# GRU layers: input weights combined on the chip, and PSUM sums with the column as the outer index

## The reference, cut to what matters

```
xn   = layernorm(x) * g + b                      # 96 channels
x_inner, z = split(xn @ w_in.T)                  # 192 + 192
gx   = x_inner @ wih.T + bih                     # for each of 4 GRUs, 3 gates of 96
step: gh = h @ whh.T + bhh
      r, u = sigmoid(gx_r + gh_r), sigmoid(gx_u + gh_u)
      n = tanh(gx_n + r * gh_n);  h = (1 - u) * n + u * h
y    = silu(fwd + bwd) * silu(z)
out  = x + y @ w_out.T
```

## Time and profile before

| | |
|---|---|
| median of 3 runs | 1262.82 us (1260.11 to 1264.99) |
| profiled execution, time | 1265.31 us |
| profiled execution, span in the profile | 1263.5 us |
| mean granted TensorE clock | 0.58 of 2.4 GHz |
| TensorE matmuls busy | 1142.3 us (90%) |
| VectorE busy | 943.2 us (75%) |
| ScalarE busy | 670.5 us (53%) |
| POOL busy | 129.8 us (10%) |

### The profile page before, as it was taken

One profiled execution on the slowest core, in us unless ns is written; L12 is line 12 of the kernel. 1 busy time (PEld: TensorE's weight loads), 2 busy tenths in 40 slices (PEclk: granted clock), 3 DMA queues, 4 the chain that ended last, 5 costly groups with the idle time before them and its releaser, 6 DMA issues. The chain is left out here.

```text
span 1263.5 us, 60733 instructions
## 1 busy us (share of the span) xinstructions
PE 1142.3 (90%) x24696; PEld 991.4 (78%) x24696; DVE 943.2 (75%) x5715; ACT 670.5 (53%) x4263; POOL 129.8 (10%) x100
## 2 busy tenths in 40 slices
PE   3778799748999999999999967999999999999995
PEld 2545254344999999999999964799999999999985
DVE  4553799964777777777777785677777777777776
ACT  4223601016666666666666652666666666666663
POOL 1001299740000000000000002000000000000000
PEclk8587799957555555555555555755555555555555
DMA  4000000000000000000000000000000000000000
GB/s 115 2 12 1 31 28 27 27 19 1 5 4 4 4 4 4 4 4 4 4 4 4 5 2 7 3 4 4 4 4 4 4 4 5 4 4 4 4 4 26
DMA packets 7955, 12.94 MB, mean 10 GB/s; under 512 B 5649, under 2 KB 6833, under 8 KB 7384
## 3 DMA queue, kind: packets, MB, share of 16 engines
q1 hardware_dynamic: 7674, 9.06, 2.3%
HBM read 8.27 MB, written 0.79 MB: 7 GB/s over the span
## 5 line engine op out<-in xcount | busy, mean ns | idle before, releaser
L1107 PE MATMUL L3s_early<-L3s_h_hi,L_w_hidden 97*128 97x8 f16 x4096 | 200.2, 175 | 4.9 <-DVE L3s_h_hi L1019 4.0
L1107 PE MATMUL L2s_early<-L2s_h_hi,L_w_hidden 97*128 97x8 f16 x4096 | 200.2, 176 | 4.8 <-DVE L2s_h_hi L1019 4.1
L1107 PEld LDWEIGHTS L3s_early<-L3s_h_hi,L_w_hidden 97*128 97x128 f16 x4096 | 163.7, 109 | 26.2 <-DVE L3s_h_hi L1019 7.8
L1107 PEld LDWEIGHTS L2s_early<-L2s_h_hi,L_w_hidden 97*128 97x128 f16 x4096 | 163.7, 109 | 25.9 <-DVE L2s_h_hi L1019 7.4
L1019 DVE TENSOR_TENSOR_SCAN L3s_h_hi<-L3s_renew,L3s_terms 96x32 f16<-96x32 f32 x512 | 113.2, 221 | 85.2 <-ACT L3s_terms L1059 59.4
L1019 DVE TENSOR_TENSOR_SCAN L2s_h_hi<-L2s_renew,L2s_terms 96x32 f16<-96x32 f32 x512 | 113.1, 221 | 85.2 <-ACT L2s_terms L1059 59.4
L1059 ACT ACTIVATE L2s_terms<-L2s_cand 96x16 f32<-96x16 f32 x512 | 111.7, 218 | 93.8 <-DVE L2s_cand L1004 62.4
L1059 ACT ACTIVATE L3s_terms<-L3s_cand 96x16 f32<-96x16 f32 x512 | 111.7, 218 | 93.7 <-DVE L3s_cand L1004 62.7
L1053 ACT ACTIVATE L2s_reset<-L2s_early 96x16 f32<-96x16 f32 x512 | 92.6, 181 | 68.3 <-PE L2s_early L1107 62.7
L1053 ACT ACTIVATE L3s_reset<-L3s_early 96x16 f32<-96x16 f32 x512 | 92.6, 181 | 68.2 <-PE L3s_early L1107 62.6
L1107 PE MATMUL L3s_early<-L3s_h_lo,L_w_hidden 96*128 96x8 f16 x2048 | 127.3, 171 | 0.1
(11 more groups left out here) (229 smaller groups left out, 2884.5 us busy)
## 6 DMA issues: line engine op xcount, KB each, us to landing
L_w_input_raw<-in_L_wih SPq DMA_DIRECT2D x2, 1164.0 KB
l_w_raw<-in_L_w SPq DMA_DIRECT2D x1, 1296.0 KB
L_w_hidden_raw<-in_L_whh SPq DMA_DIRECT2D x2, 582.0 KB
stream<-in_x SPq DMA_DIRECT2D x2, 384.0 KB, 3.6
out<-stream SPq DMA_DIRECT2D x4, 192.0 KB, 2.1
l_idft<-in_idft SPq DMA_DIRECT2D x1, 400.0 KB
rpe_lw<-in_rpe_lw SPq DMA_DIRECT2D x1, 384.0 KB
l_dft<-in_dft SPq DMA_DIRECT2D x1, 288.0 KB, 3.0
```

The lines of the kernel that those rows point to most:

```text
L1107: return e.matmul(dst, weights.hidden[0:rows, wp, GATES * (2 * g + j) + gate, :], rhs, start=False, stop=False, skip_group_check=True)
```

## The change

The input projection and the GRUs' input weights are both linear, so their product is made once per layer: `inner` (192 by 96) times `wih` gives weights that act on the normalised input directly. TensorE makes that product at the start of `gru_input`, in three PSUM banks with two fp32 products each. ScalarE rounds a bank to fp16, TensorE subtracts the rounded part with a product by minus the identity, and ScalarE rounds what is left. `forward` and `backward` hold the normalised input, with 96 channels instead of 192, so 36 input products per eight steps remain of the 72. All three kinds of sum, and `xT`, `forward`, `gate` and `y` too, have the column (batch) as outer and the step as inner index. `WeightSplit` rounds only the recurrent weights and a row of biases; the loads ask for 96 rows and for the 97th apart.

```diff
 class WeightSplit:
     def load(self, e, d):
-        for raw, name, _ in self.raw:
-            e.dma_start(raw[:], d[name]).then_inc(self.loaded, 16)
+        e.dma_start(self.hidden_raw[0:C], d[f"{self.layer}_whh"][0:C]).then_inc(self.loaded, 16)
+        e.dma_start(self.hidden_raw[C:C + 1], d[f"{self.layer}_whh"][C:C + 1]).then_inc(self.loaded, 16)
+        e.dma_start(self.bias_raw[C:C + 1], d[f"{self.layer}_bih"]).then_inc(self.loaded, 16)
+        e.dma_start(self.weights.raw[:], d[f"{self.layer}_wih"]).then_inc(self.weights.raw_loaded, 16)
+        e.dma_start(self.weights.inner[:], d[f"{self.layer}_w_inner"]).then_inc(self.weights.raw_loaded, 16)
     def lo(self, e):
-        for i, (raw, _, parts) in enumerate(self.raw):
-            e.wait_ge(self.hi_ready, i + 1)
-            e.tensor_tensor(parts[:, 1], raw[:], parts[:, 0], ALU.subtract).then_inc(self.lo_ready, 1)
+        e.wait_ge(self.hi_ready, 1)
+        e.tensor_tensor(hidden[:, 1], self.hidden_raw[:], hidden[:, 0], ALU.subtract).then_inc(self.lo_ready, 1)
+        e.wait_ge(self.hi_ready, 2)
+        e.wait_ge(self.lo_ready, 1)
+        e.tensor_tensor(bias[:, 1], self.bias_raw[C:C + 1], bias[:, 0], ALU.subtract).then_inc(self.lo_ready, 1)
+        e.wait_ge(self.lo_ready, 2)
...
 gru_input, VectorE:
+                for k in range(NB):
+                    e.wait_ge(hi_ready, k + 1)
+                    e.tensor_tensor(flat(forward[0:C, 1])[:, k * BANK:(k + 1) * BANK], xT[:, k * BANK:(k + 1) * BANK],
+                                    flat(forward[0:C, 0])[:, k * BANK:(k + 1) * BANK], ALU.subtract).then_inc(lo_ready, 1)
                 for part in range(2):
-                    for m in range(CHUNKS):
-                        e.tensor_copy(backward[0:C, part, m, 0:SEQ, :], forward[0:C, part, m, SEQ - 1::-1, :]).then_inc(reversed_, 1)
+                    e.tensor_copy(backward[0:C, part], forward[0:C, part, :, SEQ - 1::-1]).then_inc(reversed_, 1)
 gru_input, ScalarE:
+                e.activation(minus[:], ident[0:C, 0:C], ACT.Copy, scale=-1.0).then_inc(minus_ready, 1)
+                for b in range(W_BANKS):
+                    e.wait_ge(w_product, b + 1)
+                    e.activation(part_of(0, b), banks[4 + b][0:C, :], ACT.Copy).then_inc(w_hi_ready, 1)
+                for b in range(W_BANKS):
+                    e.wait_ge(w_rest, b + 1)
+                    e.activation(part_of(1, b), banks[4 + b][0:C, :], ACT.Copy).then_inc(w_lo_ready, 1)
                 for k in range(NB):
                     e.wait_ge(turned, 4 * k + 4)
-                    e.activation(xT[:].rearrange("p t b -> p b t")[:, 2 * k:2 * k + 2, :],
-                                 banks[k][0:C, :].rearrange("p (b t) -> p b t", b=2), ACT.Identity,
+                    e.activation(xT[:, k * BANK:(k + 1) * BANK], banks[k][0:C, :], ACT.Identity,
                                  scale=affine[:, 0:1], bias=affine[:, 1:2]).then_inc(scaled, 1)
+                    e.activation(flat(forward[0:C, 0])[:, k * BANK:(k + 1) * BANK], banks[k][0:C, :], ACT.Identity,
+                                 scale=affine[:, 0:1], bias=affine[:, 1:2]).then_inc(hi_ready, 1)
 gru_input, TensorE:
+                e.wait_ge(weights.raw_loaded, 32)
+                for b in range(W_BANKS):
+                    for m in range(CHUNKS):
+                        last = e.matmul(banks[4 + b][0:C, :], weights.inner[:, m, :], weights.raw[:, m, b * BANK:(b + 1) * BANK],
+                                        start=(m == 0), stop=False, skip_group_check=True)
+                    last.then_inc(w_product, 1)
+                e.wait_ge(minus_ready, 1)
+                for b in range(W_BANKS):
+                    e.wait_ge(w_hi_ready, b + 1)
+                    e.matmul(banks[4 + b][0:C, :], minus[:], part_of(0, b), start=False, stop=True,
+                             skip_group_check=True).then_inc(w_rest, 1)
                 transposes(e, norm, ident, banks, turned)
...
+                e.wait_ge(w_lo_ready, W_BANKS)
                 for i, (m, k) in enumerate(order):
+                    if m == 0:
+                        e.wait_ge(scaled, k + 1)
                     if i >= 4:
+                        e.wait_ge(gate_ready, i - 3)
-                    e.matmul(banks[4 + i % 4][0:C, :], w_in[:, m * C:(m + 1) * C], x_all[:, k * BANK:(k + 1) * BANK],
+                    e.matmul(banks[4 + i % 4][0:C, :], w_gate[:, m * C:(m + 1) * C], xT[:, k * BANK:(k + 1) * BANK],
...
 gru_steps:
-        cand_sum = lambda g, p: early[g][p][:, 1:3].rearrange("p a s c -> p (a s c)").rearrange("p (s c k) -> p s c k", c=PER, k=2)
+        cand_sum = lambda g, p: early[g][p][:, 1:3].rearrange("p a c s -> p (a c) s").rearrange("p (c k) s -> p c k s", k=2)
-                    e.tensor_tensor_scan(flat(cand[g][:, x]), flat(reset[g][:, x]), flat(cand_sum(g, p)[0:C, s]), 0.0,
+                    e.tensor_tensor_scan(flat(cand[g][:, x]), flat(reset[g][:, x]), flat(cand_sum(g, p)[0:C, :, :, s]), 0.0,
-                        e.activation(reset[g][:, x, :, 1], reset_sum(g, p)[0:C, s], ACT.Sigmoid).then_inc(activated[g], 1)
+                        e.activation(reset[g][:, x, :, 1], reset_sum(g, p)[0:C, :, s], ACT.Sigmoid).then_inc(activated[g], 1)
                         def share(dst, gate, first):
-                            for m in range(CHUNKS):
-                                rows = C + 1 if m else C
-                                for wp, xp in ((0, 0), (1, 0), (0, 1)):
+                            for wp, xp in ((0, 0), (1, 0), (0, 1)):
-                            dst = (reset_sum(g, p)[:, s, mine], keep_sum(g, p)[:, s, mine], cand_sum(g, p)[:, s, mine, 0])[gate]
+                            dst = (reset_sum(g, p)[:, mine, s], keep_sum(g, p)[:, mine, s], cand_sum(g, p)[:, mine, 0, s])[gate]
...
 gru_output, VectorE:
-                    e.tensor_tensor(y[:, m, half_of(h)], hist[g0][:, half_of(h), j0, :], mirrored[:, half_of(h)],
+                    e.tensor_tensor(y[:, m, :, half_of(h)].rearrange("p b t -> p t b"), hist[g0][:, half_of(h), j0, :], mirrored[:, half_of(h)],
-                    e.tensor_tensor(s_tok[:, m].rearrange("p b t -> p t b")[:, half_of(h), :], y[:, m, half_of(h), :],
-                                    gate[:, m, h * P * BATCH:(h + 1) * P * BATCH].rearrange("p (t b) -> p t b", b=BATCH),
+                    e.tensor_tensor(s_tok[:, m, :, half_of(h)], y[:, m, :, half_of(h)],
+                                    gate[:, m].rearrange("p (b t) -> p b t", b=BATCH)[:, :, half_of(h)],
```

More of the change, by code:

```diff
@@ L824, in __init__ @@
         n = len(GRUS) * GATES
-        layer = weights.layer
-        hidden_raw = ctx.enter_context(nc.sbuf_tensor(f"{layer}_w_hidden_raw", [C + 1, n, P], F32))
-        input_raw = ctx.enter_context(nc.sbuf_tensor(f"{layer}_w_input_raw", [C + 1, CHUNKS, n, P], F32))
-        self.raw = ((hidden_raw, f"{layer}_whh", weights.hidden), (input_raw, f"{layer}_wih", weights.input))
+        layer = self.layer = weights.layer
+        self.weights = weights
+        self.hidden_raw = ctx.enter_context(nc.sbuf_tensor(f"{layer}_w_hidden_raw", [C + 1, n, P], F32))
+        self.bias_raw = ctx.enter_context(nc.sbuf_tensor(f"{layer}_bias_raw", [C + 1, n, P], F32))
         self.loaded = ctx.enter_context(nc.semaphore(f"{layer}_w_raw_loaded"))
@@ L880, in gru_input @@
                                                                     sem("filled"), sem("reversed"))
+        minus_ready, w_product, w_hi_ready = sem("minus_ready"), sem("w_product"), sem("w_hi_ready")
+        w_rest, w_lo_ready = sem("w_rest"), sem("w_lo_ready")
         norm = Norm(nc, ctx, f"{layer}n", stream, rows, 1e-5, stats)
         banks = [ctx.enter_context(nc.psum_tensor(f"{layer}i_bank{i}", [P, BANK], F32)) for i in range(8)]
-        order = [(m, k) for m in range(CHUNKS) for k in range(NB)] + [(CHUNKS + m, k) for m in range(CHUNKS) for k in range(NB)]
-        INNER = CHUNKS * NB
+        order = [(m, k) for k in range(NB) for m in range(CHUNKS)]
+        part_of = lambda part, b: weights.input[0:C, part].rearrange("p n q -> p (n q)")[:, b * BANK:(b + 1) * BANK]
         with nc.Block() as block:
@@ L896, in _ @@
                 for x in (forward, backward):
-                    for part in range(2):
-                        e.memset(x[C:C + 1, part, 1, :, :], 1.0 - part).then_inc(filled, 1)
-                e.wait_ge(filled, 4)
+                    e.memset(x[C:C + 1, 0], 1.0).then_inc(filled, 1)
+                e.wait_ge(filled, 2)
             @block.vector
@@ L966, in gru_steps @@
         h_lo = pairs("h_lo", [C, 2, PER], F16)
[L967 to L968 removed]
+        early = [[ctx.enter_context(nc.psum_tensor(f"{layer}s_early{g}{p}", [P, 4, PER, STEPS], F32)) for p in range(2)] for g in range(GROUPS)]
+        late = [[ctx.enter_context(nc.psum_tensor(f"{layer}s_late{g}{p}", [P, 4, PER, STEPS], F32)) for p in range(2)] for g in range(GROUPS)]
         reset_sum = lambda g, p: early[g][p][:, 0]
[L970 removed]
```

(3 more changed lines are left out.)

100 lines of the change are left out of this document (46 added, 54 removed).

## The result

The changed kernel takes 1244.84 us (median of 4 runs, 1241.24 to 1248.56) against 1261.46 us for the kernel before (4 runs, 1259.80 to 1264.99): a ratio of 0.986, 95% interval 0.9841 to 0.9879. The forecast was 1240.3 with a range of 1232 to 1256. The two profiled spans are 1263.5 and 1241.1 us, so the traces can be set against each other stage by stage. A stage begins here with VectorE's first instruction of its block; the burst begins with the first weight load of an input product, the loop with the first one of a hidden product. All are differences of such starts.

The account below looks back on a forecast made before the run. VectorE's fixed order and ScalarE's functions were taken to bound the GRU loops, not TensorE. Terms summed as -2.7 - 2 x (8.5 + 1.4) = -22.5 us from the median of 1262.82, giving 1240.3, range 1232 to 1256.

Parts of the forecast that it names:

- Step 1: The GRU loop: input products fall from 72 to 36 per eight steps on TensorE alone, worth 0 us.
- Rival B: TensorE sets the GRU step, which would fall to 1.61 us: 41 us more gain, 1199; chance 0.06.
- rival A: Loop's candidate scans pay for wide PSUM reads: +21 us (1262) or +41 (1281); chance 0.07 slower, 0.07 no change.
- the rule of lines: PSUM has lines of 8 bytes; an access crossing to a new line pays, so the candidate scan's reads would too.
- The 0.63 us of the chain: Group 1's first weight load to reset Sigmoid in one loop step; its whole path takes 1.61 us, 0.08 slack.
- Step 2: End of the convolution layer: POOL's late 6 us vanish, VectorE loses 3.3 more beside POOL; -2.7 us.
- Step 3: Input stage, once a layer: 21.9 us instead of 30.5, rounded to a gain of 8.5 each.
- rival C: The clock falls or stays low in the new input stage: 6.7 us a layer, 13.4 in all, 1254; chance 0.15.
- D: The stages don't shorten; only bursts (2.8) and the convolution layer's end (2.7) gain: 1257; chance 0.03.
- Step 4: First burst of a layer: 36 input products instead of 72, a gain of 1.4 us each.
- Step 5: Output stage: the wide step moves from gate product to sum of directions, 3.68 and 2.36 us swap; 0, within 0.3.
- the ring: Seven VectorE and ScalarE starts in one loop step, no TensorE instruction among them, closing at 1.69 us, the step.

Follow-up runs that it names:

- pe_twice: The changed kernel with every input product issued twice, so 72 per eight steps again: 1248.04 us.
- ring_long: The changed kernel with one unused 16-column VectorE subtraction per step between rest(0) and candidate(1): 1286.56 us.
- ring_short: The changed kernel without the subtraction in rest, the state's low part left zero: 1216.67 us.
- steps_outer: The changed kernel with PSUM's old layout alone put back, step outer and column inner: 1248.42 us.
- no_pool_split: The changed kernel without POOL's four subtractions in the convolution layer, ScalarE writing zeros instead: 1229.97 us, ratio 0.9747.
- fill_gap: The changed kernel with three more TensorE products, result unused, in the wait for the first gate Silu: 1240.24 us, ratio 0.9824.
- after_again: The changed kernel once more, without any edit, beside other experiments: 1244.14 us, ratio 0.9863.

## Why the prediction was right, and where it was not

**Step 1, the loop: right, and by the stated mechanism.** Halving the input products gave nothing through TensorE. pe_twice puts the load back at no cost, ring_long charges 0.086 us a step for one VectorE instruction, ring_short finds the next floor at 1.63 to 1.65 where 1.61 was read. Rival B falls with these, and rival A with the scans' unchanged 200 ns: the price that the rule of lines, quoted in the prediction, would put on the scan's reads is not there. (A's own upper price was read too high: 3.32 / 3 less 2.12 / 4 us over 512 elements is 1.13 ns and not 1.2 to 1.3.) The few ns of wide hidden products are there and hidden: in the late sums they take 174 ns where they take 168 in steps_outer. The 0.63 us of the chain came from one step; over 70 steps between 400 and 520 us the way from weight load to reset Sigmoid is 0.66 before and 0.64 after, so the slack was nearer 0.05 than 0.08, which fits the 1.63 to 1.65. The loops' -1.4 and -0.3 were not predicted. The ordinary step is 1.69 in both traces, but in every 32 steps two are longer: 2.04 and 1.76 us before, 1.93 and 1.73 after in L2, 2.04 and 1.76 after in L3. Summed, the excess over 1.69 is 3.4 us before, 2.3 after in L2 and 3.4 in L3, which is most of L2's 1.4. What makes those steps longer is open.

**Step 2, the end of the convolution layer: the mechanism right, its sizes a little off.** VectorE's idle time at the end of the block falls from 6.35 to 0.61 us, 5.7 for the predicted 6.0. The extra hold-up is 2.35 us instead of 3.3, because the kernel before already paid 11.0 and not 9.1 for its two subtractions. Together that is -3.4 for the forecast's -2.7. The other 1.5 us of the -4.9 lie ahead of the 18 products, which start at 229.52 instead of 231.05, and are no part of this step. That start moves between executions: in the eleven traces of kernels that are alike up to L2's input stage (the changed kernel's two and nine experiments) the stage starts between 270.4 and 276.0. It goes with TensorE's clock early on. In the five traces with 0.98 to 1.00 between 138.5 and 146 us it starts at 270.4 to 273.2, in the six with 0.50 to 0.62 at 274.8 to 276.0. The kernel before has one trace, at 0.50. The windows of the kernel before and after, in this order:

```profile
138.50:146.00 7.50, 6.73 (x9) 2.38 (x9) 3.31 (x2) 5.15 (x8) 2.87 (x5) 0.50 0.06 27
```

```profile
138.50:146.00 7.50, 6.95 (x15) 1.97 (x15) 2.73 (x3) 6.19 (x11) 2.16 (x4) 1.00 0.99 234
```

The Trainium skill ("SBUF — State Buffer", section "Who interferes with whom") says that a VectorE instruction with two inputs in SBUF contends with a GpSimd instruction that reads SBUF, and that the one which comes second blocks fully. By that rule VectorE loses at most POOL's whole time: the 13.3 us for 12.8 come near it, while the kernel before's 11.0 are 1.9 more than POOL's 9.1. In both kernels the stretched product starts over 2 us ahead of POOL's first subtraction, so which of the two came first the records leave open. POOL's diagonals (L671), which also read SBUF, ran beside the same kind of product without such stretches (512 columns took 737 ns beside them at 237.20 in no_pool_split and 736 ns after POOL's end at 249.27 in the changed kernel); what sets them apart is not shown by any run.

**Step 3, the input stage: the chain right, the clock wrong.** The failed term is "four gate products of 0.86": it let the clock rise once and stay. It fell after TensorE's gap of 2.92 us, and the second four products took 5.34 us instead of 3.67. fill_gap takes away that alone. Counted as the prediction counts, from the end of the layer before (272.17), its stage lasts 22.4 us, 0.5 more than the predicted 21.9. This is rival C in a small form: it gave the clock's fall 3.4 us at that place, and it cost 1.7 in most stages, 2.7 to 2.9 in some and nothing in two. In the trace of after_again L3's stage took 25.5 us, 2.7 more than in the first trace: its products at the head took 8.73 instead of 7.14 and its last four 6.46 instead of 5.34. Such stages are part of what the medians lack against the forecast. (The prediction says that only A and B lie outside its range; D, at 1257, does too.) Two terms had other sizes. The eight paired copies are spaced 0.66 us and not 0.59 and take 5.5 us (282.78 to 288.24) instead of 4.7, of which the head of the stage gives back 0.2; that makes up fill_gap's 0.5. The reversed copies take 0.6 each, the lower bound, where 2.4 was taken:

```profile
288.98 1.29 DVE L919 COPY L_backward<-L_forward 96x2048 f16<-96x2048 f16 x2
```

They are hidden at either price: ScalarE's last Silu ends at 296.24.

**Step 4, the burst: right**, -1.2 for -1.4, and it ends on VectorE's memsets, as the wait in front of the hidden product shows (DVEq). **Step 5, the output stage: right**; 3.74 and 2.50 stand where 2.36 and 3.68 stood:

```profile
734.25 3.74 DVE L1175 TENSOR_TENSOR L2o_y<-L_states 96x1024 f32<-96x1024 f32 x2 [0.55 <-PEq L998]
737.83 2.50 DVE L1180 TENSOR_TENSOR L2o_s_tok<-L2o_y,L_gate 96x1024 f32<-96x1024 f32 x2
```

So the large change, half of the loop's input products, is worth nothing where it is largest. Most of its gain, 13.3 of the 22.4 us between the traces, comes from the two short input stages, where six fp32 products replace eight and VectorE's rows lie under them; the rest comes from the bursts (2.5), the end of the convolution layer (3.4), and what differs between executions.

## What to carry to other kernels

Ask for the ring, not for the busiest engine: at 99.7% busy TensorE was hidden, and the seven starts of one step told it. Then look at the short serial stages outside the loops; three edits there (a table loaded early, two kinds of ScalarE work interleaved, helpers' subtractions moved off POOL) gave 23 us, more than the 17 of the change itself. An idle engine is not free help while its instructions hold back the one on the critical path.

## What was not expected of the hardware

- Products whose result is thrown away, in a gap of 2.92 us, save 1.7 us in a stage by keeping the granted clock at 1.00 (5.34 to 3.67 us for four products), 3.9 us between the medians of two chips. Without them the clock fell behind that gap in 16 of 18 stages.
- A POOL subtraction on one row holds VectorE back as one on 97 rows does (3.08 us each), and VectorE itself needs 1.75 us for one row and 1.74 for 97.
- The stretch of VectorE's product begins before POOL's subtraction is recorded: the one of 256 columns that starts at 232.89, over 2 us ahead of POOL's 235.15, needs 0.5 us elsewhere and took 5.62. Why is open.
- A reversed fp16 copy of 2048 columns takes 0.6 us, and reads of PSUM at a step of 32 bytes take what reads side by side take.
- A one-column memset on VectorE costs 0.01 us of issue, a 16-column subtraction 0.09.
